# Attention scores and weighted sums on a Trainium2 core: both row halves of TensorE used in turn, and the value projection set between two halves of the weighing

## The reference

```
def attn_layer(x, Wqkv, qs, ksc, Wo):
    q, k, v = split(x @ Wqkv)                  # 16 heads of 64
    q = rotate(l2norm(q) * qs); k = rotate(l2norm(k) * ksc)
    # each window of 32 tokens sees itself and the window before it
    sim = einsum('bhwie,bhwje->bhwij', bq, bk2) * QK_SCALE, masked
    out = einsum('bhwij,bhwje->bhwie', softmax(sim), bv2)
    return out @ Wo
def ffn_layer(x, ...):
    return a * gelu(gate) @ W2 + b2            # a, gate = layernorm(x) @ W1 + b1
```

## Time and profile before

| | before |
|---|---|
| median of 3 runs | 3765.02 us (3751.99 to 3771.12) |
| profiled execution, time | 3765.29 us |
| its span | 3763.4 us |
| TensorE matmuls busy | 3518.5 us (93%), 64040 |
| VectorE busy | 2815.9 us (75%) |
| ScalarE busy | 2481.3 us (66%) |
| GpSimd busy | 2731.2 us (73%) |
| granted TensorE clock, mean | 0.968 |

### The profile page before, as it was taken

How to read it: one execution, slowest core, us unless ns; L and a number is a source line. 1 busy time by engine, 2 the same in 40 slices (tenths; PEclk the granted TensorE clock), 3 DMA queues, 4 the chain that set the end, 5 groups by cost and what they waited for, 6 DMA issues and landing times. The chain is left out here.

```text
span 3763.4 us, 152445 instructions
## 1 busy us (share of the span) xinstructions
PE 3518.5 (93%) x64040; PEld 2704.0 (72%) x64040; DVE 2815.9 (75%) x4959; ACT 2481.3 (66%) x3080; POOL 2731.2 (73%) x2152
## 2 busy tenths in 40 slices
PE   6999999999999999998677999999999999999996
PEld 4777777777777777776335777777777777777774
DVE  4778778777878787876446877877878787777884
ACT  4677667776777676765125766776767776777773
POOL 5877877887887787785007887778778777887771
PEclk8999999999999999999888999999999999999998
DMA  3332332332332232332002322332332332332221
GB/s 91 78 81 76 76 81 77 79 80 73 79 86 73 72 88 68 80 84 61 6 0 64 83 75 74 82 80 74 81 82 73 77 87 72 77 83 70 74 67 33
DMA packets 207416, 272.69 MB, mean 72 GB/s; under 512 B 55701, under 2 KB 101649, under 8 KB 206737
## 3 DMA queue, kind: packets, MB, share of 16 engines
q1 hardware_dynamic: 206736, 262.94, 27.0%
HBM read 60.35 MB, written 1.05 MB: 16 GB/s over the span
## 5 line engine op out<-in xcount | busy, mean ns | idle before, releaser
L1237 POOL TENSOR_TENSOR V<-RAWQK,TAB 128x512 f32<-128x512 f32 x768 | 964.6, 1279 | 619.5 <-PE PS L338 603.6
L386 PE MATMUL PS<-WH,XH 128*128 128x512 f32 x1152 | 524.1, 455 | 36.2 <-POOL XL L1217 29.5
L1263 POOL TENSOR_TENSOR V<-V,U 128x1024 f32<-128x1024 f32 x192 | 454.2, 2366 | 29.0 <-POOL V L1237 2.2
L388 PE MATMUL PS<-WL,XH 128*128 128x512 f32 x1152 | 468.0, 406 | 0.4 <-issue 0.4
L387 PE MATMUL PS<-WH,XL 128*128 128x512 f32 x1152 | 467.7, 406 | 0.8 <-issue 0.8
L1279 POOL TENSOR_TENSOR V<-V,U 128x1024 f32<-128x1024 f32 x192 | 455.1, 2371 | 15.2
L441 PEld LDWEIGHTS PS<-KT,QT 64*32 64x32 f32 x24576 | 366.5, 107 | 134.6 <-issue 134.2
L441 PE MATMUL PS<-KT,QT 64*32 64x64 f32 x24576 | 437.0, 218 | 19.1 <-issue 18.5
L471 PEld LDWEIGHTS PS<-V,PT 64*32 64x32 f32 x24576 | 342.2, 107 | 156.5 <-issue 152.3
L338 PEld LDWEIGHTS PS<-EYE,V 128*128 128x128 f32 x3072 | 348.8, 140 | 118.3 <-issue 116.1
L471 PE MATMUL PS<-V,PT 64*32 64x64 f32 x24576 | 382.2, 219 | 42.8 <-issue 41.2
(11 more groups left out here) (162 smaller groups left out, 7258.4 us busy)
## 6 DMA issues: line engine op xcount, KB each, us to landing
V<-VS SPq DMA_DIRECT2D x3072, 64.0 KB
ROTB<-c_rot SPq DMA_DIRECT2D x192, 128.0 KB, 2.5
WSTAGE<-wqkv SPq DMA_DIRECT2D x33, 512.0 KB, 4.4
WO<-wo SPq DMA_DIRECT2D x12, 512.0 KB, 3.8
W<-w SPq DMA_DIRECT2D x12, 341.0 KB, 3.2
QKS<-qks SPq DMA_DIRECT2D x12, 128.0 KB, 3.7
W<-w SPq DMA_DIRECT2D x12, 114.0 KB
VS<-wqkv SPq DMA_DIRECT2D x2, 512.0 KB, 4.4
```

Of the source, the lines that this page charges most:

```text
L386: pe.matmul(o, XH[:, p, :], WH[:, w, cols], start=True, stop=False)
L388: mm = pe.matmul(o, XH[:, p, :], WL[:, w, cols], start=False, stop=True)
L1237: ins = pool.tensor_tensor(paired(V[:, k])[:, :, :, h * half:(h + 1) * half], split(RAWQK[:, k])[:, :, :, (1 - h) * half:(2 - h) * half], ...
L1263: pool.tensor_tensor(V[:, 0], V[:, 0], U[:, 0], ALU.add).then_inc(q_turned, 1)
```

## The change

Three edits in TensorE's program, and one each in ACT's and POOL's:

- `score_half` and `weigh_half` no longer take one r. They take half of the head pairs (four of eight) and, inside, alternate r from one matmul to the next. Both masks are written one behind the other before all scores. The waits that stood ahead of each half stand once, ahead of the first. DVE still waits for both halves of the weighing and of the scores.
- `values` stands between `weigh_a` and `weigh_b`; `ffn_second` stands ahead of `ffn_third`. Some waits in `after` lists are named twice or moved, for the banks that both halves now use.
- ACT: `square_keys` stands ahead of `exponentials`. POOL: `low_part(t)` and `add_keys` stand ahead of `table`. DVE and SP keep their order.

```
-                def score_half(c, r):
-                    pe.matmul(PS[:, B_S + r, :], EYEB[:, :], rep(MASK[:, 1 if c % CH == 0 else 0, :], [P, NP_, 2 * WIN], 1),
-                              start=True, stop=False, skip_group_check=True)
+                def score_half(c, half):
+                    for j in range(half * NP_ // 2, (half + 1) * NP_ // 2):
+                        for w in range(NW):
+                            for r in range(2):
+                                mm = pe.matmul(PS[WIN * w:WIN * (w + 1), B_S + r, j * 2 * WIN:(j + 1) * 2 * WIN],
+                                               QT[DH * r:DH * (r + 1), j, WIN * w:WIN * (w + 1)],
+                                               KT[DH * r:DH * (r + 1), j, WIN * w:WIN * (w + 2)],
+                                               start=False, stop=True, skip_group_check=True)
+                    mm.then_inc(scored[half], 1)
+                def scores_a(c):
...
+                    for r in range(2):
+                        pe.matmul(PS[:, B_S + r, :], EYEB[:, :], rep(MASK[:, 1 if c % CH == 0 else 0, :], [P, NP_, 2 * WIN], 1),
+                                  start=True, stop=False, skip_group_check=True)
                     pe.wait_ge(q_kept, count(inv, c))
                     pe.wait_ge(k_kept, count(inv, c))
                     held(halo_kept, count(inv, c - 1))
...
+                def weigh_half(c, half):
+                    for j in range(half * NP_ // 2, (half + 1) * NP_ // 2):
+                        for w in range(NW):
+                            for r in range(2):
+                                mm = pe.matmul(PS[WIN * w:WIN * (w + 1), B_O + r, j * DH:(j + 1) * DH],
+                                               PT[DH * r:DH * (r + 1), j, WIN * w:WIN * (w + 1)],
+                                               V2[DH * r:DH * (r + 1), c % 2, w, j * DH:(j + 1) * DH],
+                                               start=True, stop=True, skip_group_check=True)
+                    mm.then_inc(weighed[half], 1)
...
+                    ffn_second(t - 1)
                     ffn_third(t - 1)
-                    ffn_second(t - 1)
                     weigh_a(t - 3)
+                    values(t - 1)
                     weigh_b(t - 3)
-                    values(t - 1)
                     turn_outputs(t - 3)
...
                     copy_keys(t - 1)
+                    square_keys(t - 1)
                     exponentials(t - 3)
-                    square_keys(t - 1)
...
+                    add_keys(t - 2)
                     table(t)
-                    low_part(t - 1)
-                    add_keys(t - 2)
                     scale_queries(t - 2)
                     ffn(t - 1)
                     sin_queries(t - 1)
                     add_queries(t - 1)
                     sin_keys(t - 1)
+                    low_part(t)
```

More of the change, by code:

```diff
@@ L396, in queries @@
                     pe.wait_ge(xs_low, count(inv, c))
-                    after(use(o_kept, c - 3), use(o_scaled, c - 3), use(uq_done, c - 1))
+                    after(use(o_kept, c - 3), use(o_scaled, c - 3), use(o_scaled, c - 3), use(uq_done, c - 1))
                     project(0, c, B_Q).then_inc(q_raw, 1)
@@ L421, in turn_queries @@
                     pe.wait_ge(q_scaled, count(inv, c))
-                    after(use(exp_done, c - 1), second(c), use(q_kept, c - 1), second(c - 1), second(c - 2))
-                    after(use(exp_done, c - 1), third(c), use(q_kept, c - 1), third(c - 1), third(c - 2))
+                    after(use(exp_done, c - 1), use(exp_done, c - 1), second(c), use(q_kept, c - 1), second(c - 1), second(c - 2))
+                    after(use(exp_done, c - 1), use(exp_done, c - 1), third(c), use(q_kept, c - 1), third(c - 1), third(c - 2))
                     turn(lambda h: V[:, 0, 2 * h:2 * h + 2, :].rearrange("p r d -> p (r d)"), B_TQ).then_inc(q_rows, 1)
@@ L431, in turn_keys @@
                     turn(lambda h: V[:, 1, 2 * h:2 * h + 2, :].rearrange("p r d -> p (r d)"), B_TK).then_inc(k_rows, 1)
-                def score_half(c, r):
-                    pe.matmul(PS[:, B_S + r, :], EYEB[:, :], rep(MASK[:, 1 if c % CH == 0 else 0, :], [P, NP_, 2 * WIN], 1),
-                              start=True, stop=False, skip_group_check=True)
+                def score_half(c, half):
[8 more added lines that the diff above has]
+                def scores_a(c):
+                    if not live(c):
+                        return
+                    after(second(c + 1), use(q_kept, c), use(exp_done, c - 1), use(exp_done, c - 1), second(c - 1), second(c - 2))
+                    after(third(c + 1), use(q_kept, c), use(exp_done, c - 1), use(exp_done, c - 1), third(c - 1), third(c - 2))
+                    for r in range(2):
+                        pe.matmul(PS[:, B_S + r, :], EYEB[:, :], rep(MASK[:, 1 if c % CH == 0 else 0, :], [P, NP_, 2 * WIN], 1),
+                                  start=True, stop=False, skip_group_check=True)
                     pe.wait_ge(q_kept, count(inv, c))
@@ L438, in score_half @@
                     held(halo_kept, count(inv, c - 1))
[L439 to L450, removed]
                     score_half(c, 0)
@@ L479, in weigh_a @@
                         return
-                    after(use(uq_done, c + 2), use(o_kept, c - 1), use(o_scaled, c - 1))
+                    after(use(uq_done, c + 2), use(o_kept, c - 1), use(o_scaled, c - 1), use(o_scaled, c - 1))
+                    pe.wait_ge(p_kept, count(inv, c))
+                    pe.wait_ge(v2_odd if c % 2 else v2_even, v2_count(inv, c))
                     weigh_half(c, 0)
@@ L492, in turn_outputs @@
                     pe.wait_ge(o_scaled, count(inv, c))
-                    after(use(o_scaled, c), use(uq_done, c + 2), use(o_kept, c - 1))
+                    after(use(o_scaled, c), use(o_scaled, c), use(uq_done, c + 2), use(o_kept, c - 1))
                     turn(lambda h: ON[:, 2 * h:2 * h + 2, :].rearrange("p r d -> p (r d)"), B_TO).then_inc(o_rows, 1)
@@ L534, in ffn_second @@
                     if q == 1 and 0 <= g - 1 < NGR:
-                        after(use(q_kept, n - 1), use(exp_done, n - 2), second(n - 1), second(n - 2), second(n - 3))
+                        after(use(q_kept, n - 1), use(exp_done, n - 2), use(exp_done, n - 2), second(n - 1), second(n - 2), second(n - 3))
                         if (g - 1) % NG == 0:
@@ L550, in ffn_third @@
                         return
-                    after(use(q_kept, n - 1), use(exp_done, n - 2), third(n - 1), third(n - 2), third(n - 3))
+                    after(use(q_kept, n - 1), use(exp_done, n - 2), use(exp_done, n - 2), third(n - 1), third(n - 2), third(n - 3))
                     if q == 0:
```

10 lines of the change are left out of this document (removed).

## The result

| | before | changed kernel |
|---|---|---|
| median | 3764.62 us (3751.99 to 3771.12, 4 runs) | 3884.06 us (3879.79 to 3888.32, 4 runs) |
| profiled span | 3763.4 us | 3881.5 us |
| granted clock, mean | 0.968 | 0.983 |

The ratio is 1.0321, 95% interval 1.0292 to 1.0351: slower, as forecast, but by 119 us and not by 53. 3884 lies in the range of 3700 to 3900, near its upper end.

A forecast was written before the change was run, and what follows sets the result against it. TensorE's own order was taken to set the period. From 3765.3 us, +43 for the edited steps (+0.22 a round over 192 rounds), +35 for issue waits and -25 for the clock gave 3818 us, range 3700 to 3900.

The forecast's parts named there:

- The pace of alternating small matmuls, 7.1 ns throughout: Scores and weighing: alternating row halves start a matmul every 7.1 ns instead of 14.2, gaining 1.84 us a round.
- The crossing: Middle of the weighing before the change, where both row halves meet: 31 matmuls in flight in 0.1 us against 23.
- `values` between the halves: TensorE before `turn_outputs`: `values` no longer covers the wait for `scale_outputs` (ON), costing 1.56 us a round.
- The keys' copy in q = 0: TensorE before `values`: it must wait for `keep_keys` to finish, costing 0.84 us in that round only.
- Square_keys* ahead of *exponentials: ACT's later exponentials delay `turn_weights`: 1.10 us in one round of four, after gelu, and 0.11 in the others.
- Waits for issue, +35: Runs of small matmuls: fewer waits for instructions in the weighing, longer ones in the scores; 35 us more in all.
- clock, -25: TensorE's clock: denser, shorter small runs take back about half of some 55 us lost to a fallen clock.
- B: Rival, 0.24: weighing no longer runs dry, clock stays up, some 90 us gained, 3718 us; decided by issue waits under 20.
- C: Rival, 0.20: instruction supply becomes the bound, with 1.5 us waits in the scores every second round, 3892 us, or each, 4036.
- D: Rival, 0.07: the row halves do not run side by side, so the 1.84 us gain is missing, 4161 us.
- E: Rival, 0.09: nothing moves, as added waits fall on time already lost; a TensorE waiting for ON needs no instructions; 3765 us.

## Why the prediction was right in direction and short in size

- **The pace of alternating small matmuls, 7.1 ns throughout: the step that failed.** It was carried over from the upper end of the bounds (two equal streams side by side), on a crossing of 0.1 us. Measured, under 8 ns holds for some 30 matmuls at the start of a run; a half of the weighing is 0.79 us, not 0.55, and masks with scores are 1100.17 - 1098.12 = 2.05 in place of 1061.98 - 1059.29 = 2.69. The gain is 0.64 + (1.82 - 2 x 0.79) = 0.88 us a round, not 1.84: 0.96 x 192 = 184 us missing. The crossing could not show it: it lies in a run that goes at 14 ns a matmul, slower than the 8 to 12 ns of the later part of an alternating run, so by the supply reading nothing was short there, and its window holds only 31.
- ***`values` between the halves*, +1.56 a round: right.** The wait is 1.46 in nearly every round, 281 us (forecast some 270). By itself it was tested from both sides: moved back, -207 us; covered by `scores_a`, -235 us. One reading beside it was off: VectorE's norm ends 4.43 behind the weighing (1061.09 + 0.17 - 1056.83), not 4.26, so by the forecast's own terms `row_max` would have started 0.4 us late. With the longer scores it did not matter: it starts 0.34 behind them, against 0.20 before.
- **The keys' copy in q = 0, +0.84: 0.62 measured**, since `weigh_a` is longer than was taken (the times of the earlier trace rows give 0.78; no row is named for the other 0.06). The list has 41.1 us.
- ***Square_keys* ahead of *exponentials*: the 1.10 in q = 3 is right** (a wait of 1.36 in place of 0.28), the 0.11 in other rounds is not there. Together 53 us by the ratio, against 48 x 1.43 = 69 forecast.
- **The sum with these values:** 4 x (-0.88 + 1.56) + 0.62 + 1.10 - 0.26 = +4.18 per four rounds; the trace shows 73.60 - 69.40 = +4.20. That they meet so closely is partly chance: masks and scores take 2.04 to 2.15 us in these four rounds, 2.11 on average, and with that the sum is +4.4.
- **Waits for issue, +35, and clock, -25: both too unfavourable.** Waits for issue in the two lines fell from 59.7 to 30.4 us, not rose; the first stack has a clock of 1.00, where an inner stretch of before has 0.98. All disturbances together moved by -83 us in place of +10. Here the two errors had opposite signs (184 - 93 us, less some 25 for the two small waits that came out smaller), which is why the total is only 66 us off. That the time lies in the stated range is luck in this sense: with the pace alone put right the forecast would have been 3818 + 184 = 4002 us, outside the range.
- **The rivals.** B's mechanism came true in large part: 83 of its 90 us came back, and the weighing no longer runs dry (waits for issue 45.7 us with `values` behind it, 0.7 with `values` in it), though the waits for issue of the two lines, 30.4 us, miss its mark of 20. Its time did not come, because the small matmuls gave half of what it assumed. C, with growing waits for issue, is wrong for the changed kernel, and yet supply of instructions is the reading that is left for what holds the small matmuls, as a pace rather than as stops; the prediction knew only the stops. With `values` out of the way the stops come too (114 us). D is wrong: 26 starts in 0.2 us. E's time is wrong, but what it said of a TensorE that waits for ON is seen in the scores: their waits for issue are 68.1 us without the long wait and 29.7 with it. It gives back far less than the 281 us that the wait costs.

## What to carry to other kernels

Here short matmuls, each with a weight load of its own, kept the pace of two row halves side by side for some 30 of them at the start of a run and no longer; measure the pace over a whole run, not over its first tenth of a microsecond, before costing a run at the ideal. Splitting long runs of them with other TensorE work brought the fast start back, and took most of the waits for issue out of the run that was split. A step that covers another engine's latency must be priced by what stands in its place when it moves; here one line's place was worth 207 us, more than the whole packing gained.

## What was not expected of the hardware

- **A stock of 32 pairs.** In the alternating runs the fast start ends at 32 or 33 (x33 at 0.31 us, x32 at 0.21 with half the columns), whatever the columns and however often the row half changes. Without the alternation and with half the columns no such end is to be seen. The Trainium skill (TensorE: Matmul & The Clock Gate, its table of basic figures) gives TensorE a queue of 64 entries; a load and a matmul for each pair make that 32, and the trace agrees. That it is the same queue is a reading; no run changed its depth, and how fast instructions reach TensorE is in no view: supply is what is left after columns, weight loads and the order of the row halves have been ruled out.
- **Behind it, 8.6 ns a pair with 32 columns and 10.4 with 64**, over half a microsecond. In the q = 2 round shown the last 46 of the run needed 12.4 ns each, with a second slow place behind the 91st (9 starts in 0.2 us); with half the columns there is one behind the 94th (6 starts in 0.2 us). What makes these slow places was not tried.
- **Starts 6 to 8 ns apart.** The Trainium skill (same page, on the gap between matmuls) says that starts never come closer than about 25 ns, however small the matmul. The trace does not agree for matmuls in different tiles of the array, and the measurement decides: 32 matmuls of 32 columns start in 0.21 us.
- **The clock holds next to dense small runs.** With the same wait of 1.5 us in each round the mean clock is 0.915 with one-sided runs and 0.983 with alternating ones; without that wait it is 0.968 and 0.976. The alternation hid a loss that the moved step alone brings. What exactly the clock answers to was not taken apart.
- **Waits for issue go with the length of a run.** The weighing has 38 to 49 us of them in every version in which it is one run of 128, and at most 1.5 us in every version with `values` in its middle, also in the one in which TensorE hardly waits for ON (0.9). So there it is the break that does it. The alternating scores have 63 to 68 us as one run of 128 without the long wait for ON, 30 to 45 with it, and 17 to 25 as two runs of 64 around the transposes and without it: a break helps, and so does idle time ahead of the run. How the instructions get to TensorE, and what sets the length of these stops (up to 2.6 us), was not settled.
